# The last output block of a transformer layer: mean subtracted on ScalarE, scale and residual in one VectorE operation, stores by half tiles

## The chip, the cores and the metric

The kernel runs on one NeuronCore of a Trainium2 chip. Five engines take part: TensorE (PE) multiplies, VectorE (DVE) and ScalarE (ACT) work on elements, GpSimd (POOL) works on elements more slowly, and SyncE (SP) issues the transfers between HBM and the on-chip memories. The engines run their own instruction streams and wait for one another by counting semaphores. The metric is the device time of one execution in microseconds (us), the median of several runs.

## What is computed

One layer on 2048 rows of 1024 float32 values: single-head attention and a gated feed-forward part, each on normalized rows, each output normalized again and added to its input.

```
def layernorm(x, eps=1e-5):
    return (x - mean(x)) / sqrt(var(x) + eps)

x = x + layernorm(attention(layernorm(x), Wqkv, bqkv, Wo, bo))          # x1 in the kernel
xt = layernorm(x)
y = (silu(xt @ W_gate.T) * (xt @ W_up.T)) @ W_down.T                    # F = 2752 hidden
x = x + layernorm(y)                                                    # the output
```

Only the last line concerns the change: rows y of the down projection are normalized (mean subtracted, scaled by 1/sqrt(var + eps)), the residual rows x1 are added, and the sum is stored.

## The kernel before

**Stages.** Attention comes first, by tiles of 128 rows, and leaves the rows x1 in HBM (`x1_dram`). The feed-forward part then runs in two passes of 1024 rows (`P_` = 0, 1), each pass as `gates(P_)` (gate and up products) and `downs(P_)` (down products). Every matrix product is made of three TensorE products of operands split in a high and a low part (`three`, lines 339 to 343). Each pass computes two blocks of 512 rows (T = 0, 1), that is four tiles of 128 rows (`TPB` = 4) each, and each tile's 1024 columns lie in two halves of 512 (`HALF` = 2). The four quarters of a pass's output are named `YC11`, `YC12` (the halves of block T = 0) and `YC21`, `YC22` (the halves of block T = 1) and stand in the SBUF buffer `y_all[:, quarter, tile, :]`. They are made of seven products, i = 0 to 6, of 11 steps each (`KP` = 11).

**The last product.** In pass 1, products 0 to 5 run in `downs(1)`. When they are done, three quarters are complete once VectorE has made its last four additions (`d_add`, line 1720), and only `YC21` is missing: it is product 6, which accumulates in the four PSUM banks 4 to 7, `ps[:, 4 + i, :]` for tile i. Its weights and hidden values have been split ahead and lie in `last_w`, so TensorE runs product 6 tile by tile: 11 steps of three matmuls for tile 0, then for tile 1, 2 and 3 (lines 2118 to 2124), and raises `tile_done` after each. No other work is left for TensorE.

**What the other engines do meanwhile** is the subject of the change; its code stands at lines 1773 to 1818 for VectorE, 937 to 979 for GpSimd and 737 to 744 for SyncE.

- VectorE first finishes block T = 0 of this pass: statistics (`y_stats`, line 1731), `moments` (the aggregate, line 1283), `y_norm` (line 1740). Then come the statistics of the four ready halves `YC22` (`last_stats(i, 1)`, line 1791). Then for each tile i: wait for `tile_done`, statistics of the bank (`last_stats(i, 0)`), `moments`, wait for GpSimd's `rstd`, and `last_norm` on both halves (line 1795: subtract the mean, multiply by `rstd`).
- GpSimd makes `rstd` = (var + eps)^(-1/2) of each tile in two small operations (lines 758 and 761), and adds the residual rows for tiles (`sum_y`, line 940, 128x1024). For tiles 0 to 2 of the last block it adds `last_res`, and its stream has `sum_y` of tile i - 1 ahead of `rstd` of tile i. For tile 3 VectorE adds the residual itself, one operation per half (line 1818).
- SyncE stores a whole tile (512 KB) when `y_summed` says so (line 640), and tile 3 in two halves of 256 KB (line 743). The program ends when all stores have landed.
- ScalarE has nothing to do after it has split the last weights.

The order around the change is written out by hand in each engine's stream; there is no scheduler. `tiny(...)` allocates small statistics tiles.

Of the kernel before, what the change touches and what calls it, by code (L numbers as in the profile page):

```python
# [15 lines left out]
ALU = mybir.AluOpType  # L16
AX = mybir.AxisListType

P = 128
# [151 lines left out]
def transformer_block(nc, x, xt, wqkv, bqk, bv, wo, bo, wffn, out):  # L171
# [61 lines left out]
    def tiny(name, shape):  # L233
        size = 4
        for n in shape:
            size *= n
        t = at(name, small[0], shape)
        small[0] += -(-size // 32) * 32 / KB
        return t
# [5 lines left out]
    row_max = tiny("row_max", [1])  # L245
    neg_max = tiny("neg_max", [1])
    bank_sum = tiny("bank_sum", [4])
    row_sum = tiny("row_sum", [1])
    inv_sum = tiny("inv_sum", [1])

# [65 lines left out]
    xc_loaded = [sem(f"xc_loaded{i}") for i in range(7)]  # L316
    s1_done, s2_done, s3_done, s4_done = sem("s1_done"), sem("s2_done"), sem("s3_done"), sem("s4_done")
    xc_high, a11_low, xc_low = sem("xc_high"), sem("a11_low"), sem("xc_low")
    late_loaded, late_normed = sem("late_loaded"), sem("late_normed")

    rest_loaded = sem("rest_loaded")
    w_loaded = [sem("w_loaded0"), sem("w_loaded1")]
# [12 lines left out]
    def cols(i, width=P):  # L335

        return bass.ds(i * width, width) if type(i) is not int else slice(i * width, (i + 1) * width)
# [58 lines left out]
    with nc.Block() as block:  # L396

        @block.sync
        def _(sp):
# [238 lines left out]
            def store_out(P_, T, i):  # L638
                sp.wait_ge(y_summed, 8 * P_ + 4 * T + i + 1)
                sp.dma_start(out[row_block(2 * P_ + T, i), :].rearrange("p (h n) -> p h n", h=HALF),  # L640
                             y_all[:, 2 * T:2 * T + 2, i, :]).then_inc(out_stored, 16)
# [94 lines left out]
                load_operand(n)  # L736
            for i in range(TPB):
                store_out(1, 0, i)
            for i in range(TPB - 1):
                store_out(1, 1, i)  # L740
            for h in range(HALF):
                sp.wait_ge(y_summed, 15 + h + 1)
                sp.dma_start(out[S - P:S, cols(h, BANK)], y_all[:, YC21 + h, TPB - 1, :]).then_inc(out_stored, 16)
            sp.wait_ge(out_stored, 16 * (TILES + 1))
        @block.gpsimd
        def _(pool):
            pool.memset(ident[:], 0.0).then_inc(ident_cleared, 1)
# [176 lines left out]
            def sum_y(P_, T, i):  # L924
                n = 8 * P_ + 4 * T + i
                pool.wait_ge(yn_done, n + 1)
                if P_ == 1 and T == 1:
                    pool.wait_ge(last_res_loaded, 16)
                    rows = last_res[:, i, :]
                else:  # L930
                    place = (1, 2, 3, 1)[i] if T else i
                    count = (16, 32, 32, 32)[place] if P_ == 0 and T else 16
                    if P_ == 0 and T and i == 3:
                        count = 48
                    if P_ == 1:
                        count = (32, 64, 48, 48)[place]
                    pool.wait_ge(res_loaded[place], count)
                    rows = res[:, place, :]
                y = y_all[:, 2 * T:2 * T + 2, i, :]
                pool.tensor_tensor(y, y, rows.rearrange("p (h n) -> p h n", h=HALF), ALU.add).then_inc(y_summed, 1)  # L940
# [33 lines left out]
            out_block(1, 0)  # L974
            rstd_y(1, 1, 0)
            for i in range(1, TPB):
                sum_y(1, 1, i - 1)
                rstd_y(1, 1, i)
        @block.scalar
        def _(act):  # L980
# [265 lines left out]
            def downs(P_):  # L1246
                for i in range(PRODS if P_ == 0 else PRODS - 1):
                    for k in range(KP):
                        if 1 <= i < 4 and k < TPB:
                            copy_out(P_, i, k)  # L1250
                        next_high(step_alloc(P_, i * KP + k, 1))
                        if P_ == 0:
                            if i == 1 and 5 <= k < 11:
                                split_high_half(1, (A11, A12, A22)[(k - 5) // 2], (k + 1) % 2)
                            if i == 2 and k in (7, 8):
                                split_high_half(1, S1, (k + 1) % 2)
                            if i == 3 and 5 <= k < 9:
                                split_high_half(1, (S3, S2)[(k - 5) // 2], (k + 1) % 2)
                            if i == 4 and k in (7, 8):
                                split_high_half(1, S4, (k + 1) % 2)  # L1260
# [5 lines left out]
                act.copy(y_all[:, YC21, i, :], ps[:, 4 + i, :]).then_inc(c21_copied, 1)  # L1266
            gates(1)
            downs(1)
        @block.vector
        def _(dve):  # L1270
            def row_stats(norm, i, src):
# [9 lines left out]
            def moments(norm, i):  # L1281

                dve.bn_aggr(norm.moments[:, :, i], norm.stats[:, i, :, :]).then_inc(norm.moments_done, 1)  # L1283
# [376 lines left out]
            def late_norm(p, j):  # L1660
                i = late_tile(p, LATE_STATS)
                if i is not None and j == 0:
                    dve.wait_ge(late_loaded, 16 * i + 16)
                    row_stats(norm_l, 0, res[:, 1, :])
                if i is not None and j == 1:
                    stats_in(norm_l, LNT + i)
                    moments(norm_l, 0)
                i = late_tile(p, LATE_NORM)
                if i is not None and j == 0:
                    normed(norm_l, LNT + i, 0, res[:, 1, :], late_normed)  # L1670

            def last_attention_tiles(j):
                if j == 0:
# [116 lines left out]
                    src = ps[:, 4 + i, :]  # L1790
                dve.bn_stats(norm_y.stats[:, i, h, :], src).then_inc(norm_y.stats_done, 1)

            def last_norm(i, h, done=None):
                src = y_all[:, YC22, i, :] if h else ps[:, 4 + i, :]
                op = dve.tensor_scalar(y_all[:, YC21 + h, i, :], src, norm_y.moments[:, 0, i:i + 1],
                                       norm_y.rstd[:, i:i + 1], ALU.subtract, ALU.mult)
                if done is not None:
                    op.then_inc(done, 1)

            for i in range(TPB):  # L1800
                last_stats(i, 1)
            for i in range(TPB):
                last_stats(i, 0)
                dve.wait_ge(norm_y.stats_done, 2 * (8 + TPB) + TPB + i + 1)
                moments(norm_y, i)
                dve.wait_ge(norm_y.rstd_done, 8 + TPB + i + 1)
                if i < TPB - 1:
                    last_norm(i, 0)
                    last_norm(i, 1, yn_done)
                else:  # L1810
                    dve.wait_ge(last_res_loaded, 16)
                    dve.wait_ge(y_summed, 8 + TPB + TPB - 1)
                    for h in range(HALF):
                        last_norm(i, h, yn_done)
                    for h in range(HALF):
                        dve.wait_ge(yn_done, 8 + TPB + i + 1 + h)
                        y = y_all[:, YC21 + h, i, :]
                        dve.tensor_tensor(y, y, last_res[:, i, cols(h, BANK)], ALU.add).then_inc(y_summed, 1)
        @block.tensor
        def _(pe):  # L1820
            pe.wait_ge(ident_ready, 1)
# [241 lines left out]
            def transpose_late(i, g):  # L2063
                p = 4 * i + LATE_NORM + g
                if g == 0:
                    pe.wait_ge(late_normed, i + 1)
                pe.wait_ge(u2_done, p + 1)
                transposes(4 * (p % 2) + 1, KH * g, res[:, 1, :], KH).then_inc(xq_ready, 1)

# [102 lines left out]
```

## Time and profile before

| | us |
|---|---|
| median of 3 runs | 1704.75 |
| the three runs | 1702.0, 1705.07, 1704.75 |
| the profiled execution, its own time | 1702.04 |
| its span, first to last instruction or transfer | 1700.2 |

| engine | busy us | share |
|---|---|---|
| TensorE (matmul) | 1658.3 | 98% |
| VectorE | 1110.6 | 65% |
| ScalarE | 631.0 | 37% |
| GpSimd | 519.3 | 31% |

The span is what the profile shows from inside; 1.84 us of the execution's own time lie around it. TensorE is busy for nearly all of it, so what another engine does is worth time only where TensorE waits, or after TensorE has ended. All times below are us from the start of the span.

### The profile page before, as it was taken

How to read it: one execution, taken by the hardware profiler on the slowest of the kernel's cores; microseconds unless marked ns; L12 is line 12 of the kernel's file. 1: busy time of each engine (PE TensorE's matmuls, PEld its weight loads, DVE VectorE, ACT ScalarE, POOL GpSimd, SP SyncE). 2: the span in 40 equal slices, each digit the busy share in tenths (PEclk: the TensorE clock that was granted, in tenths of full speed). 3: DMA queues.
4: the chain of work that ended last, by engine and by line, in shares of the span. 5: the costliest groups of instructions: out<-in, count | busy, mean ns of one | idle time of the engine just before them, and what ended most of it. 6: DMA issues, size and time to landing. Idle time of an engine off the chain costs nothing.

```text
span 1700.2 us, 20920 instructions
## 1 busy us (share of the span) xinstructions
PE 1658.3 (98%) x7672; PEld 1376.0 (81%) x7672; DVE 1110.6 (65%) x1605; ACT 631.0 (37%) x1141; POOL 519.3 (31%) x430
## 2 busy tenths in 40 slices
PE   6899999899999999999999999999999999999997
PEld 5788888778778888888888888888888888888886
DVE  7965677676776566666656776955565555654666
ACT  3232444334633333333336644333233233344550
POOL 3520355775165444444311100611121111200005
PEclk9999999999999999999999999999999999999999
DMA  7220466876744555454579766744444454487772
GB/s 288 112 87 11 161 212 213 278 239 207 270 160 162 171 179 177 143 167 143 178 256 327 241 209 192 262 154 138 141 136 145 146 167 153 140 290 242 231 233 99
DMA packets 161665, 317.09 MB, mean 186 GB/s; under 512 B 12960, under 2 KB 41760, under 8 KB 158624
## 3 DMA queue, kind: packets, MB, share of 16 engines
q1 hardware_dynamic: 161568, 315.82, 55.7%
q8 instruction: 59, 0.97, 0.2%
q14 instruction: 38, 0.31, 0.1%
HBM read 212.21 MB, written 103.56 MB: 186 GB/s over the span
## 4 chain that ended last, share of the span: by engine, by line
PE 87%; DVE 4%; DMA 3%; POOL 3%; SPq 1%; ACT 1%; issue 1%; POOLq 0%; DVEq 0%; ACTq 0%
PE ps L341 27%; PE ps L343 27%; PE ps L342 27%; PE ps L1932 2%; PE ps L1877 2%; PE ps L1825 2%; DMA x_dram<-x_tile 1%; PE ps L1933 1%; PE ps L1878 1%; DMA x_res<-x 1%; DVE y_all L1740 1%; DMA xc_raw<-xq_dram 1%; DVE norm_x_stats L1274 0%; POOL y_all L940 0%; DMA xq_dram<-xt_odd 0%
## 5 line engine op out<-in xcount | busy, mean ns | idle before, releaser
L1293 DVE TENSOR_TENSOR slots<-w_raw,slots 128x512 fp32r<-128x512 f32 x500 | 405.9, 834 | 266.8 <-ACT slots L1108 266.6
L1108 ACT CAST slots<-w_raw 128x512 fp32r<-128x512 f32 x504 | 301.5, 621 | 472.5 <-PE ps L343 466.4
L341 PE MATMUL ps<-xc,slots 128*128 128x512 f32 x1208 | 470.9, 390 | 1.6 <-issue 1.6
L343 PE MATMUL ps<-xc,slots 128*128 128x512 f32 x1208 | 470.1, 389 | 0.0
L342 PE MATMUL ps<-xc,slots 128*128 128x512 f32 x1208 | 470.0, 389 | 0.0
L341 PEld LDWEIGHTS ps<-xc,slots 128*128 128x128 f32 x1208 | 226.7, 188 | 48.7 <-issue 2.0
L342 PEld LDWEIGHTS ps<-xc,slots 128*128 128x128 f32 x1208 | 226.8, 188 | 47.1
L343 PEld LDWEIGHTS ps<-xc,slots 128*128 128x128 f32 x1208 | 226.7, 188 | 47.1
L341 PE MATMUL ps<-slots 128*128 128x512 f32 x572 | 222.6, 389 | 0.0
L342 PE MATMUL ps<-slots 128*128 128x512 f32 x572 | 222.5, 389 | 0.0
L343 PE MATMUL ps<-slots 128*128 128x512 f32 x572 | 222.5, 389 | 0.0
L915 POOL TENSOR_TENSOR hs<-hs 128x512 f32<-128x512 f32 x22 | 34.2, 1553 | 353.5 <-DVE hs L1606 320.2
L341 PEld LDWEIGHTS ps<-slots 128*128 128x128 f32 x572 | 107.4, 188 | 22.7 <-DVE slots L1293 0.3
L343 PEld LDWEIGHTS ps<-slots 128*128 128x128 f32 x572 | 107.4, 188 | 22.3
L342 PEld LDWEIGHTS ps<-slots 128*128 128x128 f32 x572 | 107.4, 188 | 22.1
L1108 ACT CAST slots<-tt 128x512 fp32r<-128x512 f32 x84 | 52.4, 624 | 143.8 <-PE ps L343 137.8
L1932 PE MATMUL ps<-v,probs_t 128*128 128x512 f32 x256 | 94.5, 406 | 0.2 <-DVE probs_t L1293 0.2
L758 POOL TENSOR_TENSOR norm_y_var_eps<-norm_y_moments,eps 128x1 f32<-128x1 f32 x16 | 5.9, 368 | 269.5 <-DVE norm_y_moments L1283 269.5
L1293 DVE TENSOR_TENSOR slots<-tt,slots 128x512 fp32r<-128x512 f32 x84 | 70.0, 835 | 10.7 <-ACT slots L1108 10.6
L1933 PE MATMUL ps<-v,probs_t 128*128 128x256 f32 x256 | 72.6, 284 | 0.0
L830 POOL TENSOR_TENSOR tt<-w_raw 128x512 f32<-128x512 f32 x21 | 27.6, 1312 | 126.8 <-DVE slots L1293 77.6
L341 PE MATMUL ps<-k_t,q_tile 128*128 128x512 f32 x128 | 55.2, 431 | 5.0 <-DVE q_tile L1293 4.9
(181 smaller groups left out, 2405.5 us busy)
## 6 DMA issues: line engine op xcount, KB each, us to landing
w_raw<-hsp_dram SPq DMA_DIRECT2D x154, 256.0 KB, 3.7
hsp_dram<-hs SPq DMA_DIRECT2D x20, 1792.0 KB, 8.4
w_raw<-wffn SPq DMA_DIRECT2D x134, 256.0 KB, 3.5
w_raw<-wffn SPq DMA_DIRECT2D x66, 512.0 KB, 6.4
w_raw<-wdt_dram SPq DMA_DIRECT2D x88, 256.0 KB, 3.6
wgt_dram<-tt SPq DMA_DIRECT2D x21, 1024.0 KB, 8.3
w_raw<-wgt_dram SPq DMA_DIRECT2D x84, 256.0 KB, 2.8
wdt_dram<-tt SPq DMA_DIRECT2D x11, 1024.0 KB, 5.3
```

What stands on the lines that cost most here:

```text
L341: pe.matmul(dst, stat(HIGH), mov(HIGH), start=first, stop=False, skip_group_check=reread)
L342: pe.matmul(dst, stat(HIGH), mov(LOW), start=False, stop=False, skip_group_check=reread)
L343: return pe.matmul(dst, stat(LOW), mov(HIGH), start=False, stop=last, skip_group_check=reread)
L830: pool.tensor_tensor(tt[:, TT1, :], w_raw[:, raw + Q12, :], w_raw[:, raw + Q11, :], ALU.subtract).then_inc(t_ready, 1)
L915: pool.tensor_tensor(hs[:, HS3, :], hs[:, HA11, :], hs[:, HA21, :], ALU.subtract).then_inc(s_done, 1)
L1108: act.copy(operand(n, HIGH), source(n)).then_inc(w_high, 1)
L1293: return dve.tensor_tensor(dst, src, high.bitcast(F32), ALU.subtract)
L1740: dve.tensor_scalar(y, y, norm_y.moments[:, 0, i:i + 1], norm_y.rstd[:, i:i + 1], ALU.subtract, ALU.mult).then_inc(yn_done, 1)
L1825: last = pe.transpose(ps[:, bank, cols(j)], src[:, cols(k0 + j)], ident[:])
L1877: pe.matmul(bank, xn_t[:, HIGH, k, cols(i)], wv[:, k, :, :], start=k == 0, stop=False)
L1932: pe.matmul(ps[:, 6, :], probs_t[:, HIGH, k, :], v[:, k, :, :], start=k == 0, stop=False)
L1933: last = pe.matmul(ps[:, 6, 0:D], probs_t[:, LOW, k, :], v[:, k, HIGH, :], start=False, stop=k == TILES - 1)
```

## The change

For the four tiles of the last block (pass 1, T = 1):

- VectorE still makes the statistics and the aggregate. It now also writes the negative mean, `neg_mean[:, i]` (128x1), and raises `mean_negated`.
- ScalarE computes y - mean for both halves (one activation each, function Identity, with `neg_mean` as bias), the first half from PSUM, the second half in place in SBUF, and raises `yn_done` after each.
- VectorE computes (y - mean) * rstd + residual in one operation per half (`last_sum`, `scalar_tensor_tensor`), and raises `y_summed` after each.
- GpSimd no longer adds `last_res` for tiles 0 to 2; only the four `rstd` are left there.
- The waits for `last_res` and for GpSimd's sum of the block before (`y_summed` at 12) move ahead of the tile loop of VectorE. Before, they stood ahead of tile 3's norm.
- All eight half tiles are stored by themselves, 256 KB each.
- The semaphore `late_normed` of an earlier stage is merged into `x1n_done`; instructions and waits stay where they were.

```
+    neg_mean = tiny("neg_mean", [TPB])
...
-            for i in range(TPB - 1):
-                store_out(1, 1, i)
-            for h in range(HALF):
-                sp.wait_ge(y_summed, 15 + h + 1)
-                sp.dma_start(out[S - P:S, cols(h, BANK)], y_all[:, YC21 + h, TPB - 1, :]).then_inc(out_stored, 16)
-            sp.wait_ge(out_stored, 16 * (TILES + 1))
+            for i in range(TPB):
+                for h in range(HALF):
+                    sp.wait_ge(y_summed, 8 + TPB + 2 * i + h + 1)
+                    sp.dma_start(out[row_block(BLOCKS - 1, i), cols(h, BANK)],
+                                 y_all[:, YC21 + h, i, :]).then_inc(out_stored, 16)
+            sp.wait_ge(out_stored, 16 * (TILES + TPB))
...
             for i in range(1, TPB):
-                sum_y(1, 1, i - 1)
                 rstd_y(1, 1, i)
...
             downs(1)
+            for i in range(TPB):
+                act.wait_ge(mean_negated, i + 1)
+                for h in range(HALF):
+                    src = y_all[:, YC22, i, :] if h else ps[:, 4 + i, :]
+                    act.activation(y_all[:, YC21 + h, i, :], src, ACT.Identity,
+                                   bias=neg_mean[:, i:i + 1]).then_inc(yn_done, 1)
...
-                    normed(norm_l, LNT + i, 0, res[:, 1, :], late_normed)
+                    normed(norm_l, LNT + i, 0, res[:, 1, :], x1n_done)
...
-            def last_norm(i, h, done=None):
-                src = y_all[:, YC22, i, :] if h else ps[:, 4 + i, :]
-                op = dve.tensor_scalar(y_all[:, YC21 + h, i, :], src, norm_y.moments[:, 0, i:i + 1],
-                                       norm_y.rstd[:, i:i + 1], ALU.subtract, ALU.mult)
-                if done is not None:
-                    op.then_inc(done, 1)
+            def last_sum(i, h):
+                dve.wait_ge(yn_done, 8 + TPB + 2 * i + h + 1)
+                y = y_all[:, YC21 + h, i, :]
+                dve.scalar_tensor_tensor(out=y, in0=y, scalar=norm_y.rstd[:, i:i + 1],
+                                         in1=last_res[:, i, cols(h, BANK)], op0=ALU.mult,
+                                         op1=ALU.add).then_inc(y_summed, 1)
 
             for i in range(TPB):
                 last_stats(i, 1)
+            dve.wait_ge(last_res_loaded, 16)
+            dve.wait_ge(y_summed, 8 + TPB)
             for i in range(TPB):
                 last_stats(i, 0)
                 dve.wait_ge(norm_y.stats_done, 2 * (8 + TPB) + TPB + i + 1)
                 moments(norm_y, i)
+                dve.wait_ge(norm_y.moments_done, 8 + TPB + i + 1)
+                dve.tensor_scalar(neg_mean[:, i:i + 1], norm_y.moments[:, 0, i:i + 1], -1.0, None,
+                                  ALU.mult).then_inc(mean_negated, 1)
                 dve.wait_ge(norm_y.rstd_done, 8 + TPB + i + 1)
-                if i < TPB - 1:
-                    last_norm(i, 0)
-                    last_norm(i, 1, yn_done)
-                else:
-                    dve.wait_ge(last_res_loaded, 16)
-                    dve.wait_ge(y_summed, 8 + TPB + TPB - 1)
-                    for h in range(HALF):
-                        last_norm(i, h, yn_done)
-                    for h in range(HALF):
-                        dve.wait_ge(yn_done, 8 + TPB + i + 1 + h)
-                        y = y_all[:, YC21 + h, i, :]
-                        dve.tensor_tensor(y, y, last_res[:, i, cols(h, BANK)], ALU.add).then_inc(y_summed, 1)
+                for h in range(HALF):
+                    last_sum(i, h)
```

How the change moves instructions shows best on two engines. VectorE, at the end of its stream, tile 3 before (`ps` is the bank of the last product):

```order
L1791 BN_STATS norm_y_stats<-ps 128x6 [waits tile_done]
L1283 BN_AGGR norm_y_moments<-norm_y_stats 128x2 [waits norm_y_stats_done]
L1795 TENSOR_SCALAR y_all<-ps,norm_y_moments,norm_y_rstd 128x512 [waits y_summed,last_res_loaded,norm_y_rstd_done]
L1795 TENSOR_SCALAR y_all<-y_all,norm_y_moments,norm_y_rstd 128x512
L1818 TENSOR_TENSOR y_all<-y_all,last_res 128x512 [waits yn_done] x2
```

and tile 3 after:

```order
L1797 BN_STATS norm_y_stats<-ps 128x6 [waits tile_done]
L1289 BN_AGGR norm_y_moments<-norm_y_stats 128x2 [waits norm_y_stats_done]
L1815 TENSOR_SCALAR neg_mean<-norm_y_moments 128x1 [waits norm_y_moments_done]
L1802 SCALAR_TENSOR_TENSOR y_all<-y_all,norm_y_rstd,last_res 128x512 [waits yn_done,norm_y_rstd_done]
L1802 SCALAR_TENSOR_TENSOR y_all<-y_all,norm_y_rstd,last_res 128x512 [waits yn_done]
```

Four large operations have become two, and a small one that releases ScalarE stands ahead of them. GpSimd, last tiles before (`eps` and `minus_half` are constants):

```order
L940 TENSOR_TENSOR y_all<-y_all,res 128x2x512 [waits res_loaded3,yn_done]
L758 TENSOR_TENSOR norm_y_var_eps<-norm_y_moments,eps 128x1 [waits norm_y_moments_done]
L761 TENSOR_TENSOR norm_y_rstd<-norm_y_var_eps,minus_half 128x1 [waits norm_y_eps_added]
L940 TENSOR_TENSOR y_all<-y_all,last_res 128x2x512 [waits last_res_loaded,yn_done]
L758 TENSOR_TENSOR norm_y_var_eps<-norm_y_moments,eps 128x1 [waits norm_y_moments_done]
```

and after:

```order
L941 TENSOR_TENSOR y_all<-y_all,res 128x2x512 [waits res_loaded3,yn_done]
L759 TENSOR_TENSOR norm_y_var_eps<-norm_y_moments,eps 128x1 [waits norm_y_moments_done]
L762 TENSOR_TENSOR norm_y_rstd<-norm_y_var_eps,minus_half 128x1 [waits norm_y_eps_added]
L759 TENSOR_TENSOR norm_y_var_eps<-norm_y_moments,eps 128x1 [waits norm_y_moments_done]
```

No large addition stands between one tile's `rstd` and the next any more.

## Rows read from the trace of the kernel before

**Rows 1.** The profile's page: busy time by engine; 40 slices; share of the chain.

```profile
PE 1658.3 (98%) x7672; PEld 1376.0 (81%) x7672; DVE 1110.6 (65%) x1605; ACT 631.0 (37%) x1141; POOL 519.3 (31%) x430
...
ACT  3232444334633333333336644333233233344550
...
PE 87%; DVE 4%; DMA 3%; POOL 3%; SPq 1%; ACT 1%; issue 1%; POOLq 0%; DVEq 0%; ACTq 0%
```

**Rows 2.** Waits from 1658 us on: engine, line, releaser: total us, times, longest.

```profile
DVE y_all L1795 <- POOL norm_y_rstd L761: 8.2, 4, 2.4
```

**Rows 3.** Timeline of TensorE: start us, duration us; first and last matmul of product 6.

```profile
1659.76 0.39 PE L341 MATMUL ps<-last_w 128*128 128x512 f32 x1
...
1689.45 0.39 PE L343 MATMUL ps<-last_w 128*128 128x512 f32 x1
```

**Rows 4.** Timeline of VectorE, last block: start us, duration us of the group.

```profile
1679.81 0.68 DVE L1791 BATCH_NORM_STATS2 norm_y_stats<-ps 128x6 f32<-128x512 f32 x1
1680.52 0.21 DVE L1283 BATCH_NORM_AGGREGATE norm_y_moments<-norm_y_stats 128x2 f32<-128x12 f32 x1
1681.66 0.81 DVE L1795 TENSOR_SCALAR y_all<-ps,norm_y_moments,norm_y_rstd 128x512 f32<-128x512 f32 x1 [0.93 <-POOL norm_y_rstd L761]
...
1691.93 0.69 DVE L1791 BATCH_NORM_STATS2 norm_y_stats<-ps 128x6 f32<-128x512 f32 x1
1692.66 0.21 DVE L1283 BATCH_NORM_AGGREGATE norm_y_moments<-norm_y_stats 128x2 f32<-128x12 f32 x1
1695.25 0.81 DVE L1795 TENSOR_SCALAR y_all<-ps,norm_y_moments,norm_y_rstd 128x512 f32<-128x512 f32 x1 [2.37 <-POOL norm_y_rstd L761]
1695.98 0.54 DVE L1795 TENSOR_SCALAR y_all<-y_all,norm_y_moments,norm_y_rstd 128x512 f32<-128x512 f32 x1
1696.43 1.29 DVE L1818 TENSOR_TENSOR y_all<-y_all,last_res 128x512 f32<-128x512 f32 x2
```

**Rows 5.** Timeline of GpSimd in the same stretch.

```profile
1677.59 2.40 POOL L940 TENSOR_TENSOR y_all<-y_all,res 128x1024 f32<-128x1024 f32 x1 [0.63 <-DVE y_all L1740]
1680.81 0.19 POOL L758 TENSOR_TENSOR norm_y_var_eps<-norm_y_moments,eps 128x1 f32<-128x1 f32 x1 [0.82 <-DVE norm_y_moments L1283]
1681.08 0.55 POOL L761 TENSOR_TENSOR norm_y_rstd<-norm_y_var_eps,minus_half 128x1 f32<-128x1 f32 x1
...
1692.10 2.34 POOL L940 TENSOR_TENSOR y_all<-y_all,last_res 128x1024 f32<-128x1024 f32 x1 [1.38 <-DVE y_all L1795]
1694.40 0.19 POOL L758 TENSOR_TENSOR norm_y_var_eps<-norm_y_moments,eps 128x1 f32<-128x1 f32 x1
1694.66 0.55 POOL L761 TENSOR_TENSOR norm_y_rstd<-norm_y_var_eps,minus_half 128x1 f32<-128x1 f32 x1
```

**Rows 6.** Timeline of SyncE's queue; stores, KB each, us to landing.

```profile
1697.14 0.95 SPq L743 DMA_DIRECT2D out<-y_all  x2
...
out<-y_all SPq DMA_DIRECT2D x2, 256.0 KB, 2.1
```

**Rows 7.** Groups of ScalarE by shape over the whole run: count, busy us, mean ns, idle.

```profile
L1198 ACT ACTIVATE gs<-gs 128x512 f32<-128x512 f32 x62 | 38.8, 628 | 0.0
L1244 ACT COPY y_all<-ps 128x512 f32<-128x512 f32 x24 | 13.9, 577 | 0.0
L1010 ACT ACTIVATE q_t<-ps,bqk_sb 128x512 f32 x6 | 4.0, 689 | 8.3 <-PE ps L343 8.3
```

**Rows 8.** Timeline of VectorE and ScalarE in attention, one row maximum and its use.

```profile
343.91 0.16 DVE L1445 TENSOR_REDUCE row_max<-bank_max 128x1 f32<-128x4 f32 x1
344.10 0.15 DVE L1447 TENSOR_SCALAR neg_max<-row_max 128x1 f32<-128x1 f32 x1
...
344.29 0.69 ACT L1063 ACTIVATE probs<-ps,neg_max 128x512 f32<-128x512 f32 x1 [0.22 <-DVE neg_max L1447]
```

**Rows 9.** VectorE operations of two lines: duration ns min/median/max, first and last start.

```profile
L1335 DVE SCALAR_TENSOR_TENSOR k_t<-ps,bqk_sb,k_t x8: 733/743/751, 58.7 to 149.5; 128x512 f32 x4, 128x512 fp32r<-128x512 f32 x4
...
L1649 DVE TENSOR_TENSOR hs<-hs,gs x20: 692/1521/1746, 495.6 to 1462.1; 128x512 f32<-128x512 f32 x20
```

More of the change, by code:

```diff
@@ L318, in transformer_block @@
     xc_high, a11_low, xc_low = sem("xc_high"), sem("a11_low"), sem("xc_low")
-    late_loaded, late_normed = sem("late_loaded"), sem("late_normed")
+    late_loaded, mean_negated = sem("late_loaded"), sem("mean_negated")
     rest_loaded = sem("rest_loaded")
@@ L2065, in transpose_late @@
                 if g == 0:
-                    pe.wait_ge(late_normed, i + 1)
+                    pe.wait_ge(x1n_done, LNT + i + 1)
                 pe.wait_ge(u2_done, p + 1)
```

## Prediction

> **What bounds the kernel now.** I read the page first. TensorE is busy 98% of the span and makes 87% of the chain that ended last [rows 1]. The change touches nothing that TensorE waits for: it begins behind the last six products' additions, when TensorE has only product 6 left, and that product needs no other engine. So the time before TensorE's end stays, and the question is what happens from there on. Next the timeline of TensorE: product 6 starts at 1659.76 and its last matmul starts at 1689.45 and ends at 1689.84 [rows 3]. These are 132 matmuls (4 tiles x 11 steps x 3), one per (1689.45 - 1659.76) / 131 = 0.227 us, so 7.48 us a tile. The banks of tiles 0 to 3 are complete at about 1667.4, 1674.9, 1682.4 and 1689.84. The span ends at 1700.2: a tail of 10.4 us behind TensorE. This tail is all that can be won or lost.
>
> The timelines of VectorE and GpSimd show what the tail is made of. VectorE begins tile 3's statistics only at 1691.93, 2.1 us after its bank is complete [rows 3, 4]. It was late because of a ring: VectorE's norm of a tile waits for GpSimd's rstd, and GpSimd's rstd of the next tile stands behind its addition of 2.4 us [rows 5]. The waits say the same: 8.2 us in four waits for rstd [rows 2]. The norms of tiles 0 and 3 start at 1681.66 and 1695.25 [rows 4], which is 4.53 us a tile. In tile 3 itself the aggregate ends at 1692.87, but the eps addition starts at 1694.40, when the residual sum of tile 2, started at 1692.10, is through [rows 4, 5].
>
> **The change part by part, on tile 3.** I write each tile as a chain from the start t of its bank's statistics.
>
> Tile 0 of the kernel before shows the chain with nothing in GpSimd's way: statistics 1679.81, aggregate 1680.52 (+0.71), eps addition 1680.81 (+1.00), power 1681.08 (+1.27), first VectorE operation that uses rstd 1681.66 (+1.85) [rows 4, 5]. So rstd is usable at t + 1.85, and the new chain keeps this path.
>
> Beside it runs the new path through ScalarE. The nearest rows are in attention: row maximum at 343.91, its negation (the same 128x1 operation) at 344.10, the activation that has it as bias at 344.29 [rows 8]. The first link is 0.03 us behind an operation of 0.16, the second 0.19 from start to start. With the aggregate's 0.21: negative mean at t + 0.71 + 0.21 + 0.03 = t + 0.95, ScalarE at t + 1.14. Its first half, Identity from PSUM with a pointer bias, is in the trace: 0.69 us [rows 7]. It ends at t + 1.83; with 0.04 for the hand-over VectorE can start at t + 1.87. That is a tie with rstd (t + 1.85): **ScalarE's first pass is hidden under GpSimd's rstd**, and costs 0.02. If that cover were gone, it would cost its whole 0.69.
>
> The second half reads SBUF. The trace has an activation in SBUF without a pointer at 0.63; a pointer costs 0.69 - 0.58 = 0.11 by the two PSUM rows [rows 7]; so 0.63 to 0.74, and I take 0.73. It starts about 0.10 before the first ends, at t + 1.73, and ends at t + 2.46.
>
> VectorE's fused operation with two SBUF inputs is not in the trace. From below it is bounded by the plain addition of the same shape, 1.29 us for two, the second starting some 0.60 after the first, 0.69 each [rows 4]; from above by the fused operation with one PSUM input, 0.74 [rows 9]. I take 0.73, the form with its pointer operand being nearer to the second. First half t + 1.87; second half at t + 2.52 (0.65 later, and ScalarE's t + 2.50 is just in time); end t + 3.25. With the low ends this is 3.15, with the high ends 3.4.
>
> Before, the same stretch is 1695.25 to 1697.72 behind rstd: two norms and two additions, 2.47 us [rows 4]. Now it is 3.25 - 1.85 = 1.40. Gain 1.07 us.
>
> GpSimd: the addition that stood ahead of tile 3's rstd is gone. Before, the eps addition began 1694.40 - 1692.66 = 1.74 behind the start of the aggregate; free, it is 0.29 [rows 4, 5]. Gain 1.45 us.
>
> Backlog: does tile 3 start on time? A tile now holds VectorE for about 3.16 us (the next statistics can start 0.09 before the last fused operation ends), 3.1 to 3.3 with the ends above. The new wait ahead of the tile loop counts here: VectorE may not start tile 0 until GpSimd's last sum of the block before is through, 1677.59 + 2.40 = 1679.99 [rows 5], against 1679.81 before. Queued behind that wait on VectorE are all four tiles, and ScalarE and SyncE wait for them. So tile 0 starts at 1680.03, tile 1 at 1683.19, tile 2 at 1686.35, and VectorE is free at 1689.51, with 0.33 to spare before tile 3's bank is there at 1689.84. Tile 3 starts at 1689.89, where it started at 1691.93. Gain 2.04 us. The spare is thin: with a tile of 3.3 it is nearly gone, and above that each 0.1 us of a tile costs 0.4 at the end.
>
> Stores: the last half tile is ready at 1697.72, and the span ends 2.48 later, landing of 2.1 included [rows 6]. After the change the last store is the same 256 KB, with the half before it issued 0.65 earlier (0.6 before). Six more of 256 KB take the place of three of 512 KB; tile 2's last one would be issued near 1689.6, over 3 us before tile 3's first, so no transfer is in the way. Nothing gained or lost.
>
> ScalarE's stream has nothing else here: its last slice of the page is at 0 [rows 1], so the new waits stop nobody. The merged semaphore changes no instruction. The built program has no activation table load that the one before lacks.
>
> **Sum.** 2.04 + 1.45 + 1.07 = 4.56. The other way: 1689.89 + 3.25 + 2.48 = 1695.62 against 1700.2, 4.6 less. The bounds of the unknown operations give 4.3 to 4.7. The profiled execution took 1702.04 with 1.84 around its span; with the change I expect 1695.6 + 1.84 = 1697.5. It was one of the quicker ones: the median of the runs is 2.7 above it. On the median I forecast **1704.75 - 4.6 = 1700.2 us**.
>
> One rule of the Trainium skill speaks against this. The row shows VectorE's norm of the SBUF half at 0.54 us [rows 4] and ScalarE's comparable pass at 0.63 to 0.74 [rows 7]. The page "ScalarE: Activation LUTs", section Rules for kernel authors, says that additions and multiplications belong on VectorE rather than ScalarE; the page gives the reason in VectorE's higher rate per element. By it each half would be dearer by some 0.1 to 0.2 us, and if ScalarE's passes stood on the path instead of under rstd, each tile would take about 0.7 longer, tile 3 would start at 1691.6 and the gain would shrink to some 2.2. I go by the overlap with rstd, which the page doesn't weigh.
>
> **The rivals.**
> *A tile is longer than its slot.* If semaphore hops through three engines add 0.2 to 0.3 us a tile (each hop was taken from one row), a tile is 3.45: tile 3 starts at 1680.03 + 10.35 = 1690.38, its chain is 3.5, and the span ends at 1696.4. Gain 3.8; with ScalarE's first pass uncovered as well (0.69 a tile, 3.85), tile 3 starts at 1691.58, and the end is 1698.0: gain 2.2, a time of 1702.5. For it speaks the thin spare, against it that every link has a row.
>
> *The ring becomes longer than the old one: slower.* Place: VectorE's two fused operations of each tile. Both read two SBUF tiles, and one VectorE addition of that kind and size in this trace ranges from 0.69 to 1.75 us with a median of 1.52 [rows 9], beside large GpSimd operations. If the fused operations were stretched to 1.5 each, a tile would take some 4.7, and the end is 1680.03 + 3 x 4.7 + 4.8 + 2.48 = 1701.4, 1.2 more than before (1706.0 on the median). It turns from gain to loss at a tile of 4.4. Against it: GpSimd has only two 128x1 operations a tile left, and VectorE's own additions in this stretch took 0.69 [rows 4]. The Trainium skill, "Perfetto Trace Analysis", section Optimizing Scalar/DVE Operations, says that GpSimd and VectorE share an SBUF read port; the spread of that row agrees, and by that rule too the stretch needs large GpSimd work.
>
> *The tail shrinks, but the measurement hides it.* The three runs spread over 3 us. A gain of 4.6 that is drawn against runs of 1702 and 1705 can come out between 3 and 6.
>
> **Chances.** About 0.2% (3.4 us) is what a measurement of this kernel can tell from no change. The forecast, a gain of 4.3 to 4.7 in the span, has 0.74. A longer tile, with a gain of 2 to 4.2, has 0.20. No gain or a gain below 2 for another reason, 0.04; slower by the stretched operations, 0.02. The first case gives less than 3.4 on the medians one time in seven by the runs' spread, the second about one time in two. That makes faster 0.73, same 0.25, slower 0.02. The range: down by 2.7 for a median that falls on the quicker runs (1697.5), up to the gain of 2.2 (1702.5); 1697.3 to 1702.5.
>
> **What would show it.** In the changed profile: the first statistics of a bank at about 1680.0 and the last at 1689.9, right behind the last matmul; ScalarE's first activation some 1.1 behind each bank's statistics; eps additions of GpSimd 0.3 behind each aggregate; two fused operations of 0.7 to 0.75; last store issued near 1693.2, the span's end near 1695.6. Wrong would be: statistics of tile 3 well behind 1690 (the ring is the bound), fused operations over 1 us, or VectorE waiting for ScalarE rather than GpSimd by more than 0.1.

## The result

| | before | changed |
|---|---|---|
| median of 22 runs each | 1703.07 us | 1698.38 us |
| ratio, 95% interval | | 0.9973 [0.9966, 0.9981] |
| profiled execution, its own time | 1702.04 | 1698.70 |
| its span | 1700.2 | 1696.9 |
| last matmul ends (start + 0.39) | 1689.84 | 1690.93 |
| tail: span's end minus the last matmul's end | 10.36 | 5.97 |

The change makes the kernel faster by 0.27%, with an interval of 0.19 to 0.34%: 4.6 us of 1703.07. One of the 22 runs of the kernel before took 2802.43 us and is not among the fast runs that the ratio compares. The forecast was 1704.75 - 4.6 = 1700.2. The difference came out as forecast; the level is 1.8 lower, nearly all of it because the median of more runs of the kernel before is 1703.07, not 1704.75.

In the two profiles the spans differ by only 3.3 us, because product 6 began 1.08 us later in the changed kernel's execution (1660.84 against 1659.76), in a part of the program that is the same in both. Over the eleven profiles of this study it began anywhere between 1657.4 and 1661.6, and the ten kernels with the merged semaphore lie on both sides of the kernel before. The tail leaves that scatter out, and from here on I compare tails: 10.36 - 5.97 = 4.39 us won, against 1700.2 - 1695.62 = 4.58 forecast. The spans are given to 0.1 us, so one tail is good to about 0.05 us; starts and durations are given to 0.01.

### The profile page after: what moved, and what is told of

Same layout as the page of the kernel before. It is cut to its first block, busy times and chain, and to the rows that moved or that the text cites. A ratio compares the mean times of both kernels' runs of the same rounds, so it can differ in the third digit from the quotient of the medians.

```text
span 1696.9 us, 20931 instructions
## 1 busy us (share of the span) xinstructions
PE 1658.4 (98%) x7672; PEld 1376.1 (81%) x7672; DVE 1110.7 (65%) x1607; ACT 636.7 (38%) x1149; POOL 512.2 (30%) x427
## 4 chain that ended last, share of the span: by engine, by line
PE 85%; DVE 5%; DMA 4%; POOL 2%; issue 1%; ACT 1%; SPq 1%; DVEq 0%; POOLq 0%; ACTq 0%
PE ps L342 26%; PE ps L344 26%; PE ps L343 26%; PE ps L1933 2%; PE ps L1826 2%; PE ps L1878 1%; DMA x_dram<-x_tile 1%; PE ps L1934 1%; PE ps L1879 1%; DMA x_res<-x 1%; DMA w_raw<-hsp_dram 1%; DMA xc_raw<-xq_dram 1%; DVE y_all L1746 1%; DVE norm_x_stats L1280 0%; DMA xq_dram<-xt_odd 0%
```

## The profile after

First the page of the changed kernel, busy time by engine and the chain that ended last, to be read against [rows 1]:

```profile
PE 1658.4 (98%) x7672; PEld 1376.1 (81%) x7672; DVE 1110.7 (65%) x1607; ACT 636.7 (38%) x1149; POOL 512.2 (30%) x427
...
PE 85%; DVE 5%; DMA 4%; POOL 2%; issue 1%; ACT 1%; SPq 1%; DVEq 0%; POOLq 0%; ACTq 0%
```

TensorE is what it was, GpSimd has lost 7.1 us (three additions), ScalarE has gained 5.7 (eight passes), VectorE is where it was. No page of busy times would show that anything was won.

The timeline of TensorE, last matmul, as in [rows 3]; start us, duration us:

```profile
1690.54 0.39 PE L344 MATMUL ps<-last_w 128*128 128x512 f32 x1
```

The timeline of VectorE, tile 0, tile 1's statistics and tile 3, as in [rows 4]:

```profile
1681.19 0.70 DVE L1797 BATCH_NORM_STATS2 norm_y_stats<-ps 128x6 f32<-128x512 f32 x1 [0.19 <-issue]
...
1684.48 0.69 DVE L1797 BATCH_NORM_STATS2 norm_y_stats<-ps 128x6 f32<-128x512 f32 x1
...
1691.05 0.69 DVE L1797 BATCH_NORM_STATS2 norm_y_stats<-ps 128x6 f32<-128x512 f32 x1
1691.77 0.21 DVE L1289 BATCH_NORM_AGGREGATE norm_y_moments<-norm_y_stats 128x2 f32<-128x12 f32 x1
1692.02 0.15 DVE L1815 TENSOR_SCALAR neg_mean<-norm_y_moments 128x1 f32<-128x1 f32 x1
1693.00 1.41 DVE L1802 SCALAR_TENSOR_TENSOR y_all<-y_all,norm_y_rstd,last_res 128x512 f32<-128x512 f32 x2 [0.82 <-ACT y_all L1273]
```

ScalarE in tile 3, then GpSimd in tile 3, as in [rows 5]:

```profile
1692.21 0.69 ACT L1273 ACTIVATE y_all<-ps,neg_mean 128x512 f32<-128x512 f32 x1 [1.99 <-DVE neg_mean L1815]
1692.79 0.71 ACT L1273 ACTIVATE y_all<-y_all,neg_mean 128x512 f32<-128x512 f32 x1
```

```profile
1692.06 0.19 POOL L759 TENSOR_TENSOR norm_y_var_eps<-norm_y_moments,eps 128x1 f32<-128x1 f32 x1 [2.46 <-DVE norm_y_moments L1289]
1692.33 0.55 POOL L762 TENSOR_TENSOR norm_y_rstd<-norm_y_var_eps,minus_half 128x1 f32<-128x1 f32 x1
```

What to see. A tile now takes 1684.48 - 1681.19 = 3.29 us, where the norms of the tiles lay 4.53 apart. Tile 3's statistics begin 0.12 us behind the last matmul, where it was 2.09. GpSimd's eps addition starts 0.29 behind the aggregate, where it was 1.74. Behind the first use of rstd came 2.47 us of VectorE work, now the two fused operations take 1.41. And the wait for rstd of [rows 2] is gone; in its place the waits of the changed kernel (engine and line, releaser: us in total, times, longest) list

```profile
DVE y_all L1802 <- ACT y_all L1273: 3.3, 4, 0.8
```

so it is ScalarE, by a little, that VectorE waits for last: rstd was ready at 1692.33 + 0.55 = 1692.88, ScalarE's half at 1692.90, the fused operation began at 1693.00. In these 0.10 us lies a semaphore instruction of its own in VectorE's queue, which carries the wait for ScalarE. The chain that ended last has it (start us, duration us):

```profile
1692.93 0.02 DVEq L1800
```

## Experiments

All were measured on their tails, each in its own profile; where a ratio is given, it is to the kernel before, on the same chip. To read them together: t is the start of the statistics of a tile's bank, and a tile's time is the distance from one tile's t to the next, without the last distance where tile 3 waits for TensorE. In two kernels tile 0 is shorter than the others, because no addition of the last block stands in its way on GpSimd: 3.04 in the kernel before, 3.24 in the one where GpSimd keeps its sums. The table has their other tiles; the 4.53 of the kernel before is the distance of its norms, and its statistics lie 4.55 and 4.53 apart.

| kernel | a tile, us | last matmul ends | span | tail |
|---|---|---|---|---|
| before | 4.53 | 1689.84 | 1700.2 | 10.36 |
| changed | 3.29 | 1690.93 | 1696.9 | 5.97 |
| VectorE alone, no fused operation | 4.26 | 1691.16 | 1701.0 | 9.84 |
| GpSimd keeps its sums | 4.10 | 1690.77 | 1699.7 | 8.93 |
| GpSimd kept busy | 4.22 | 1687.46 | 1697.1 | 9.64 |
| one more ScalarE pass | 3.87 | 1689.56 | 1697.8 | 8.24 |
| VectorE subtracts early, no ScalarE | 3.36 | 1690.23 | 1696.5 | 6.27 |
| whole stores, tiles 0 to 2 | 3.29 | 1691.33 | 1697.3 | 5.97 |
| whole stores, all tiles | 3.29 | 1691.71 | 1698.7 | 6.99 |
| head wait moved | 3.28 | 1689.80 | 1695.7 | 5.90 |
| head wait moved, waits swapped | 3.27 | 1690.52 | 1696.4 | 5.88 |

### GpSimd freed, but VectorE does everything in the old order

```
-            (ScalarE's passes and the negative mean)
...
                 dve.wait_ge(norm_y.rstd_done, 8 + TPB + i + 1)
+                for h in range(HALF):
+                    dve.tensor_scalar(y_half, src, mean, rstd, ALU.subtract, ALU.mult)
                 for h in range(HALF):
-                    (fused scale and residual)
+                    dve.tensor_tensor(y_half, y_half, last_res_half, ALU.add)
```

> The GpSimd part of the change alone: GpSimd makes only rstd for the last four tiles, VectorE subtracts and scales both halves and adds the residual for every tile, ScalarE does nothing. I measure the tail, from the end of the last matmul to the end of the span: 10.36 us in the kernel before, 5.97 in the changed one. Ring theory (the parts pay only together, since the tile time must fit into what TensorE leaves): a tile takes 1.85 to rstd plus 0.73 + 0.45 + 0.61 + 0.60 = 4.24 us, tile 3's statistics start about 3.0 us behind the last matmul, its chain is 4.3, the tail 9.8 us, so only 0.6 of the 4.4 us are won. Rival (the parts add up): freeing GpSimd gives back the 1.74 - 0.29 = 1.45 us that tile 3's rstd waited and all of the backlog of 2.1 us, tail 6.8 to 8.9 us.

Tail 9.84 us; ratio 0.9994 [0.9985, 1.0004], not told from no change. The ring theory's 9.8 was met. The timeline of VectorE in this kernel, last tile:

```profile
1694.19 0.69 DVE L1791 BATCH_NORM_STATS2 norm_y_stats<-ps 128x6 f32<-128x512 f32 x1
...
1696.06 0.81 DVE L1809 TENSOR_SCALAR y_all<-ps,norm_y_moments,norm_y_rstd 128x512 f32<-128x512 f32 x1 [0.93 <-POOL norm_y_rstd L762]
1696.78 0.54 DVE L1809 TENSOR_SCALAR y_all<-y_all,norm_y_moments,norm_y_rstd 128x512 f32<-128x512 f32 x1
1697.24 1.28 DVE L1796 TENSOR_TENSOR y_all<-y_all,last_res 128x512 f32<-128x512 f32 x2
```

GpSimd is out of the way (the wait is 0.93 in every tile, no 2.4 any more), yet tile 3 starts 3.0 us behind the last matmul. The work only changed from GpSimd to VectorE, which is in the same ring.

### ScalarE subtracts, but GpSimd keeps its sums

```
             for i in range(1, TPB):
+                pool.wait_ge(scaled, i)
+                pool.tensor_tensor(y, y, last_res of tile i - 1, ALU.add)
                 rstd_y(1, 1, i)
...
                 dve.wait_ge(norm_y.rstd_done, 8 + TPB + i + 1)
+                if i < TPB - 1:
+                    dve.wait_ge(yn_done, 8 + TPB + 2 * i + 2)      # both of ScalarE's halves
+                    dve.tensor_scalar(y, y, rstd, None, ALU.mult).then_inc(scaled, 1)
+                    continue
```

> The ScalarE part of the change alone: ScalarE subtracts the mean, VectorE only scales tiles 0 to 2 (128x1024), and GpSimd adds their residual ahead of the next tile's rstd as before; tile 3 as in the changed kernel. Ring theory: the ring of scale, GpSimd's addition of 2.4 us and rstd stays, about 4.1 us a tile, tile 3's statistics start late and its rstd waits for the addition of tile 2; tail 8.9 us (1.4 won of 4.4). Rival (the parts add up): only the 1.07 us of VectorE's own shorter chain are won, tail 9.3 us, or, if ScalarE is what shortened the ring, tail near 6.5.

Tail 8.93 us, as the ring theory had it; ratio 0.9996 [0.9985, 1.0006]. GpSimd in this kernel, around tile 3:

```profile
1692.70 2.34 POOL L981 TENSOR_TENSOR y_all<-y_all,last_res 128x1024 f32<-128x1024 f32 x1 [0.93 <-DVE y_all L1826]
1695.00 0.19 POOL L760 TENSOR_TENSOR norm_y_var_eps<-norm_y_moments,eps 128x1 f32<-128x1 f32 x1
1695.27 0.55 POOL L763 TENSOR_TENSOR norm_y_rstd<-norm_y_var_eps,minus_half 128x1 f32<-128x1 f32 x1
```

The two halves of the change, each alone, win 0.52 and 1.43 us of the tail; together 4.39. (The first of them also leaves out the fused operation, and subtracts behind the wait for rstd; the run in which VectorE subtracts early shows what these two are worth together.)

### One more ScalarE pass in each tile

```
                 act.wait_ge(mean_negated, i + 1)
+                act.activation(w_raw[:, 3, :], ps[:, 4 + i, :], ACT.Identity, bias=neg_mean[:, i:i + 1])
```

The added pass writes a scratch tile that nothing reads.

> The changed kernel with one more ScalarE pass over the PSUM half into a scratch tile ahead of the two real ones, in each of the last four tiles: 0.59 us more before the first half is ready. Ring theory: there is no slack left in the ring, so the cost counts in all four tiles: tail 5.97 + 4 x 0.59 = 8.3 us. Rival (TensorE's end sets tile 3's start and only tile 3's own chain counts): tail 5.97 + 0.59 = 6.6 us. If the first pass had slack under rstd, less than either.

Tail 8.24: 2.27 us for a pass that delays the half by 0.58 to 0.59, a factor of 3.9; ratio 0.9989 [0.9977, 1.0001]. The tile went from 3.29 to 3.87. The rival, that only tile 3's chain counts, would have had 6.6. So in the changed kernel the ring still has no slack: what a tile costs in addition is paid four times.

### GpSimd kept busy beside the fused operations

```
             for i in range(TPB):
                 rstd_y(1, 1, i)
+                pool.tensor_tensor(w_raw[:, 2, :], w_raw[:, 0, :], w_raw[:, 1, :], ALU.add)
```

The addition is on scratch tiles and nothing waits for it.

> The changed kernel with one more GpSimd addition of 128x512 on scratch tiles behind each of the last four rstd, so that it runs beside VectorE's two fused operations; nothing waits for it, and it is through before the next rstd if it takes its usual 1.3 us. Shared-port theory: the fused operations stretch from 0.75 to 1.4 to 1.75 us, a tile takes 4.5 or more, tail about 11 us, at or above that of the kernel before. Rival (the fused operation is not slowed by GpSimd, the long rows of the other line had another cause): fused operations 0.75, tail 6.0.

Tail 9.64; ratio 1.0003 [0.9990, 1.0015]. The kind of effect is the shared-port theory's, its size was put too high. The fused operations of this kernel (ns min/median/max), then VectorE and GpSimd in tile 3:

```profile
L1802 DVE SCALAR_TENSOR_TENSOR y_all<-y_all,norm_y_rstd,last_res x8: 739/1200/1692, 1679.7 to 1693.9; 128x512 f32<-128x512 f32 x8
```

```profile
1692.31 2.33 DVE L1802 SCALAR_TENSOR_TENSOR y_all<-y_all,norm_y_rstd,last_res 128x512 f32<-128x512 f32 x2 [0.82 <-ACT y_all L1273]
```

```profile
1692.16 1.27 POOL L978 TENSOR_TENSOR w_raw<-w_raw 128x512 f32<-128x512 f32 x1
```

A GpSimd addition of 1.27 us stretches the pair from 1.41 to 2.33, by 0.92, and is not slowed itself (1.26 to 1.29 in the four tiles). It began 0.15 us ahead of the fused operation. The second fused operation, begun when GpSimd is done, is at 0.74 again; that is why my 1.5 for each was too much. Nothing waits for that addition, no semaphore joins it to anything, and it takes back 3.67 of the 4.39 us. The forecast's mechanism for a loss is real, then; it needed large GpSimd work beside these operations, and the change itself removes that. The run shows the stretch; that the cause is a port is not shown by it.

Two more things stand in the trace of the kernel before, and both widen this. A VectorE operation with a single SBUF input is stretched too. The norm of a whole tile of block T = 0, once with no large GpSimd work beside it, and once beside GpSimd's addition of 1674.57, 2.39 us long:

```profile
1664.94 0.80 DVE L1740 TENSOR_SCALAR y_all<-y_all,norm_y_moments,norm_y_rstd 128x1024 f32<-128x1024 f32 x1
...
1674.63 2.87 DVE L1740 TENSOR_SCALAR y_all<-y_all,norm_y_moments,norm_y_rstd 128x1024 f32<-128x1024 f32 x1 [0.93 <-POOL norm_y_rstd L761]
```

The four statistics of SBUF halves behind it took 0.67 to 0.68 us each, 2.46 in all, though three of them began beside the next such addition (1677.59, 2.40); they are not stretched. And it is not always VectorE that pays. GpSimd adds 128x512 tiles at line 835 21 times: the 14 additions that began while VectorE was idle took 1.28 to 1.30 us, the 7 that began while a VectorE operation on SBUF operands ran took 1.74 to 1.75. In both directions the engine that started second was the slow one.

### VectorE subtracts early, ScalarE out

```
                 dve.wait_ge(norm_y.moments_done, 8 + TPB + i + 1)
-                dve.tensor_scalar(neg_mean[:, i:i + 1], ..., -1.0, None, ALU.mult).then_inc(mean_negated, 1)
+                for h in range(HALF):
+                    dve.tensor_scalar(y_half, src, norm_y.moments[:, 0, i:i + 1], None, ALU.subtract)
                 dve.wait_ge(norm_y.rstd_done, 8 + TPB + i + 1)
                 for h in range(HALF):
                     last_sum(i, h)
```

> The changed kernel without ScalarE: VectorE subtracts the mean from both halves itself, right behind the aggregate and before it waits for rstd, and then runs the same fused operations; no negative mean is made. This asks what ScalarE is worth once GpSimd is free and the scale and residual are fused. Idle-gap theory: in the changed kernel VectorE sits idle for 0.82 us a tile anyway, so its own subtractions (0.73 + 0.46 us by the kernel before) cost little: first subtraction at +0.96, fused operations at +2.15 and +2.80, end +3.55 against +3.36, a tile 3.46 against 3.29; tile 3 starts 0.64 us behind the last matmul; tail 6.7 us, so ScalarE is worth 0.7 of the 4.4 us. Rival (ScalarE's parallel pass is the change's main part): a tail of 8 us or more.

Tail 6.27, better than the 6.7 expected; ratio 0.9979 [0.9967, 0.9990]. VectorE in tile 3:

```profile
1690.55 0.70 DVE L1791 BATCH_NORM_STATS2 norm_y_stats<-ps 128x6 f32<-128x512 f32 x1
...
1691.52 0.75 DVE L1811 TENSOR_SCALAR y_all<-ps,norm_y_moments 128x512 f32<-128x512 f32 x1
1692.19 0.48 DVE L1811 TENSOR_SCALAR y_all<-y_all,norm_y_moments 128x512 f32<-128x512 f32 x1
1692.59 1.41 DVE L1796 SCALAR_TENSOR_TENSOR y_all<-y_all,norm_y_rstd,last_res 128x512 f32<-128x512 f32 x2
```

No gap is left: VectorE subtracts in the time in which it had sat waiting for rstd, and the fused pair starts at t + 2.04 instead of t + 1.95. With one operation and one pointer operand the passes took 0.75 and 0.48, not the 0.81 and 0.54 of the norms with two of each [rows 4], on which the 6.7 was built. So ScalarE is worth 0.30 us of the 4.39; four times the 0.07 by which the tiles differ is 0.28. The rest, from 10.36 to 6.27, comes from three things on VectorE and GpSimd: no sums on GpSimd, the subtraction ahead of the wait for rstd, and scale and residual in one operation. Against the first experiment, in which GpSimd is just as free, the last two of them take a tile from 4.26 to 3.36 and the tail from 9.84 to 6.27: 0.90 a tile, 3.57 in all, four times as much again. No run has one of these two without the other, but the rows say what the fused operation is worth by itself. The two subtractions take 1692.59 - 1691.52 = 1.07 us here and the fused pair 1.41, together 2.48; the norms and additions of the first experiment take 1697.24 + 1.28 - 1696.06 = 2.46. By this estimate fusing saves nothing: it is worth something only because it leaves a subtraction that needs no rstd and can stand ahead of the wait.

### Stores

```
             for i in range(TPB):
+                if i < K:                  # K = 3 in one kernel, 4 in the other
+                    (one store of the whole tile behind its second half)
+                    continue
                 for h in range(HALF):
```

> The changed kernel with the stores of tiles 0 to 2 undone: whole tiles of 512 KB, tile 3 still in two halves. If these stores lie beside the ring and only the last store counts: tail (end of last matmul to end of span) 5.97 us as in the changed kernel, within 0.05. Rival (more, smaller stores keep SyncE or the queues busier, or let the transfers clear earlier): a tail that differs by 0.2 us or more.

> All four tiles of the last block stored whole, 512 KB each. The last landing of a half tile took 2.0 us and that of a whole tile 3.1 us, so if the last store's size counts in full: tail 7.0 us. Rival (a landing is mostly a fixed time and the halves follow each other anyway): tail 6.3 us or less.

Tails 5.97 and 6.99. Storing tiles 0 to 2 by halves, which is the new part of the stores in this change, is worth nothing that the profile can show. Tile 3 by halves, which the kernel before had already, is worth 1.02. Of these two kernels and the next there is one execution each, so I read only their tails. The landing of the stores (issues, KB each, us to landing) in the second kernel and in the changed one:

```profile
out<-y_all SPq DMA_DIRECT2D x8, 512.0 KB, 3.1
```

```profile
out<-y_all SPq DMA_DIRECT2D x8, 256.0 KB, 2.0
```

### The wait at the head, and the order of two waits

```
-            dve.wait_ge(y_summed, 8 + TPB)         # ahead of the tile loop
...
+                if i == 0:                          # behind tile 0's negative mean
+                    dve.wait_ge(y_summed, 8 + TPB)
+                dve.wait_ge(yn_done, 8 + TPB + 2 * i + 1)   # second kernel only: ahead of the wait for rstd
```

> The changed kernel with VectorE's wait for GpSimd's sum of the block before moved from ahead of the tile loop to behind tile 0's negative mean. Tile 0's statistics start 0.27 us earlier. If TensorE's end is the floor for tile 3, only the 0.07 us that the ring was late come back: tail 5.90 us. Rival (the ring alone sets tile 3's start): tail 5.70 us.

> As the one before, and VectorE waits first for ScalarE's half and then for rstd, instead of the other way round. In the changed kernel 0.10 us lie between the end of ScalarE's first pass and the fused operation, with a semaphore instruction of 0.02 in VectorE's queue among them; where one wait was enough it was 0.04. If the order of the two waits is what costs 0.06: tail 5.84 us. Rival (an instruction with two waits costs the same in either order): 5.90. Against the kernel before the time should be 4.5 us lower either way, a ratio of 0.9974.

Tails 5.90 and 5.88; the second kernel's ratio is 0.9972 [0.9962, 0.9983]. In the first, VectorE is through with tile 2 in time and starts on tile 3 when the last matmul allows it (last matmul 1689.41 + 0.39 = 1689.80):

```profile
1689.84 0.70 DVE L1797 BATCH_NORM_STATS2 norm_y_stats<-ps 128x6 f32<-128x512 f32 x1
```

Tile 0 starts 0.29 us earlier against the last matmul (10.03 instead of 9.74 ahead of its end), but only 0.08 come back: tile 3 starts 0.04 behind the last matmul instead of 0.12, and from there TensorE is the floor.

Swapping the two waits takes 0.01 off a tile, and the fused operation still starts about 0.09 behind the last release. That doesn't show that the order is all the same. The swap puts the wait for rstd into the semaphore instruction and the wait for ScalarE's half on the operation itself, but both are released within 0.02 us of each other, so by these rows whichever stands in the semaphore instruction is paid for. Where the two releases lie far apart, the difference shows: with one more ScalarE pass the semaphore instruction has the late wait, 0.6 us behind rstd, and the fused operation starts 0.10 behind it (1693.83, 1693.93). Where GpSimd keeps its sums, ScalarE is done 0.9 us before rstd, the operation itself has the late wait, and tile 1's scale starts 0.03 behind rstd's end (1687.67, 1687.70), with two waits all the same. So the order would matter if one release came clearly first; no run here has that with the waits swapped.

This is the fastest tail of the study, 0.09 us better than the changed kernel's, far below what timed runs can tell (0.9972 against 0.9973).

## Why the prediction was right

**Place and size.** The change was costed on the tail alone, as three terms. Measured in the same way, on the distances within each profile:

| term | forecast | measured |
|---|---|---|
| tile 3 starts on time (backlog) | 2.04 | 2.09 - 0.12 = 1.97 |
| rstd no longer behind GpSimd's sum | 1.45 | 1.74 - 0.29 = 1.45 |
| behind rstd: from 2.47 to | 1.40, so 1.07 | (3.36 - 1.85) = 1.51, so 0.96 |
| store and end | 0 | 2.48 and 2.49, 0 |
| sum | 4.56 | 4.38 |

**What was a little off.** The tile was put at 3.16 and takes 3.29. Half of that is the hand-over to the fused operation, for which the forecast had no row of its own: 0.04 where the late wait is on the operation itself, 0.10 here, where it stands in a semaphore instruction ahead of it, so the pair starts at t + 1.95 instead of t + 1.87. The rest is a few hundredths each: the statistics of a bank, the fused operation (0.75, at the upper of its two bounds) and its step of 0.67. The forecast gave VectorE 0.33 us to spare before tile 3. Three tiles of 0.13 more use all of it, tile 0 itself started 0.07 later against the last matmul than forecast (9.74 ahead of its end, not 9.81), and tile 3 came 0.07 to 0.08 late. The spare hid most of the error: without it 0.13 in a tile would have cost 0.5. The forecast said that above a tile of 3.3 each tenth costs four; by the measured starts that edge is at 3.26, so the kernel stands 0.03 beyond it, and the added ScalarE pass shows the slope from there.

**ScalarE "hidden under rstd".** Nearly: it is the later of the two by 0.02, plus the hand-over. The forecast did not ask whether ScalarE was needed at all. That part was missing rather than wrong: I let the change's gain stand as one package, and the run with VectorE alone, subtracting early, got 4.09 of the 4.39.

**The rule against ScalarE.** The pass over the SBUF half takes 0.71 on ScalarE and 0.48 on VectorE, the pass over the PSUM half 0.69 and 0.75. The Trainium skill, page "ScalarE: Activation LUTs", section Rules for kernel authors, would keep such work on VectorE; the gain that it names is for bf16, and these tiles are float32. For the SBUF half the trace agrees, for the PSUM half it does not; and what decided was neither, but that VectorE had 0.82 us of idle time per tile in which to do it. With the subtraction kept on VectorE, as that rule has it, the gain was 4.09 instead of 4.39, not the 2.2 that I gave it: I had put the passes on the path, as if VectorE could not do them while it waited.

**The rivals.** The longer tile (0.20) was the one that came closest, at 3.29 for the 3.45 it asked for. The slower ring (0.02) did not come about, but its mechanism did as soon as GpSimd was given work. The stores behaved as costed, nothing for tiles 0 to 2.

**One line for the kernels whose four tiles are alike.** In the five of them with the head wait and the last tile stored by halves, tile 0 starts 9.73 to 9.76 us ahead of the last matmul's end. Three tiles follow, then tile 3's chain, which is a tile and 0.06 to 0.09, and 2.46 to 2.50 for the store. So the tail is about 4 times the tile minus 7.18: 9.86, 9.70, 8.30, 6.26 and 5.98 for tiles of 4.26, 4.22, 3.87, 3.36 and 3.29, measured 9.84, 9.64, 8.24, 6.27 and 5.97. The kernel in which GpSimd keeps its sums is not on the line (9.22 for a tile of 4.10, measured 8.93), because its tile 0 is shorter and its tile 3 waits longer for rstd. By the same starts the line ends at a tile of (9.74 + 0.04) / 3 = 3.26, where TensorE becomes the floor.

The 9.74 itself is not TensorE's doing: tile 0's bank is complete over 22 us before the last matmul ends, and VectorE comes to it late because of the block before, three of whose norms took 2.74, 2.73 and 2.87 us beside GpSimd's additions where the first took 0.80. What it would give to free VectorE there, no run here shows.

## What to carry to other kernels

When the last stage of a kernel passes each tile around a ring of engines, find the tile time of the ring and the time that is left for it; until the ring fits, each tenth saved in a tile counts once for every tile, and moving work from one engine of the ring to another wins next to nothing. Look first at what an engine could do before it waits instead of behind it (here: subtract the mean before rstd is there), and only then for another engine to do it. And keep large GpSimd additions from running beside the VectorE operations on the path that work from SBUF to SBUF, those with two SBUF inputs and the norms with one, even where no semaphore joins them.

## What the runs showed of the hardware

- A GpSimd addition of 128x512 lengthened a pair of fused VectorE operations by 0.92 us of its 1.27, and ran at full speed itself, having started first. The Trainium skill, "Perfetto Trace Analysis", section Optimizing Scalar/DVE Operations, names the shared SBUF read port, and these numbers agree.
- A VectorE norm of 128x1024 with one SBUF input took 0.80 us without, and 2.73 to 2.87 beside, a GpSimd addition of 2.4; statistics of SBUF halves were not stretched. A GpSimd addition of 128x512 that started second took 1.74 to 1.75 instead of 1.28 to 1.30.
- A subtraction on VectorE with one pointer scalar took 0.75 (PSUM) and 0.48 (SBUF); a subtraction and multiplication in one operation, with two pointer scalars, took 0.81 and 0.54. No run separates the second pointer from the second operation.
- An Identity pass on ScalarE with a pointer bias took 0.69 from PSUM and 0.71 from SBUF. Its first use came 28.33 us after the engine's last work and cost nothing extra.
- Where the wait that was released last stood in a semaphore instruction of its own ahead of the VectorE operation, the operation started 0.09 to 0.11 us behind that release; where it stood on the operation itself, 0.03 to 0.04, with one wait or with two.
